# Macaron stack on one core: the routed experts' probability in the scattered row, and stack transfers issued one by one

## The reference

```python
logits = jnp.einsum('bsd,de->bse', x, router_w)
probs = jax.nn.softmax(logits, axis=-1)
topk_vals, topk_idx = jax.lax.top_k(probs, TOP_K)
top1_val = topk_vals[..., 0]
top1_idx = topk_idx[..., 0]
hid = jnp.einsum('bsd,edh->ebsh', x, up_w) * jax.nn.silu(jnp.einsum('bsd,edh->ebsh', x, gate_w))
mask = (top1_idx[None, :, :] == jnp.arange(Er)[:, None, None]).astype(x.dtype)
routed = jnp.einsum('ebsh,ehd,ebs->bsd', hid, down_w, mask)
...
return ALPHA * top1_val[..., None] * routed + shared
```

## Time and profile before

| | |
|---|---|
| median of 3 runs | 1754.54 us (1752.41 to 1758.84) |
| the profiled execution | 1754.69 us |
| span of its profile | 1752.7 us |
| PE busy | 1596.1 us, 91% |
| DVE busy | 969.2 us, 55% |
| ACT busy | 797.1 us, 45% |
| POOL busy | 343.7 us, 20% |
| stage m1 | 118 to 257 us of the span |
| guarded attention | 296 to 567 us |
| stage m2 | 568 to 700 us |

### The profile page before, as it was taken

How to read it: one execution, slowest core, us unless ns; L and a number is a source line. 1 busy time by engine, 2 the same in 40 slices (tenths; PEclk the granted TensorE clock), 3 DMA queues, 4 the chain that set the end, 5 groups by cost and what they waited for, 6 DMA issues and landing times. The chain is left out here.

```text
span 1752.7 us, 34539 instructions
## 1 busy us (share of the span) xinstructions
PE 1596.1 (91%) x13629; PEld 913.5 (52%) x13633; DVE 969.2 (55%) x2195; ACT 797.1 (45%) x1302; POOL 343.7 (20%) x489
## 2 busy tenths in 40 slices
PE   7979987899998998999789988999789986979998
PEld 2445654454553665445544554666434434755665
DVE  7674347887783333634563434545734446763455
ACT  5643333476675332432133334222588865643221
POOL 1313232132323322300330014000500000132000
PEclk9988998999999899999899989999999998989999
DMA  4633025111101411000000013564231004415563
GB/s 114 238 114 119 19 54 159 48 49 40 32 30 71 157 43 41 1 0 1 1 0 1 1 32 78 123 140 95 62 92 46 26 1 119 118 33 118 124 143 76
DMA packets 56305, 120.83 MB, mean 69 GB/s; under 512 B 8487, under 2 KB 35143, under 8 KB 51347
## 3 DMA queue, kind: packets, MB, share of 16 engines
q1 hardware_dynamic: 53676, 113.55, 24.1%
q0 software_dynamic: 2432, 5.00, 0.8%
q10 hardware_dynamic: 39, 0.07, 0.0%
HBM read 85.38 MB, written 19.96 MB: 60 GB/s over the span
## 5 line engine op out<-in xcount | busy, mean ns | idle before, releaser
L2512 DVE TENSOR_REDUCE a_most<-psum 128x1 f32<-128x512 f32 (+3 forms) x304 | 181.4, 654 | 45.4 <-PE psum L2142 44.2
L3407 ACT ACTIVATE t_silu<-psum 128x512 f32<-128x512 f32 x136 | 81.2, 597 | 258.2 <-PE psum L3467 257.1
L2470 ACT ACTIVATE a_probs<-psum 128x512 f32<-128x512 f32 (+1 forms) x304 | 153.9, 584 | 91.9 <-PE psum L2142 90.4
L3484 PEld LDWEIGHTS psum<-t_slot,t_hid 128*128 128x128 f32 x1024 | 131.0, 192 | 55.9 <-issue 44.7
L2773 ACT ACTIVATE ga_probs<-psum 128x1024 f32<-128x1024 f32 (+2 forms) x160 | 137.1, 954 | 19.4 <-PE psum L2142 18.8
L3583 DVE TENSOR_TENSOR t_prod<-t_silu,psum 128x512 f32<-128x512 f32 x104 | 71.4, 686 | 134.6 <-ACT t_silu L3407 125.2
L3484 PE MATMUL psum<-t_slot,t_hid 128*128 128x128 f32 x1024 | 132.0, 275 | 4.3 <-DVE t_hid L3574 4.3
L3467 PE MATMUL psum<-xnT,t_slot 128*128 128x512 f32 x256 | 131.3, 595 | 3.1 <-ACT t_silu L3407 3.1
L2142 PE MATMUL psum<-a_ks,a_qs 96*32 96x512 bf16 (+3 forms) x1536 | 123.9, 340 | 10.9 <-issue 5.6
L3472 PE MATMUL psum<-xnT,t_slot 128*128 128x512 f32 x256 | 130.7, 592 | 0.0
L2142 PE MATMUL psum<-a_qs,a_ks 128*32 128x512 bf16 (+3 forms) x1536 | 116.6, 330 | 5.4 <-ACT a_probs L2470 2.3
(11 more groups left out here) (455 smaller groups left out, 2996.7 us busy)
## 6 DMA issues: line engine op xcount, KB each, us to landing
t_spread<-factors SPq DMA_DIRECT2D x64, 512.0 KB, 6.4
m_experts<-experts_dram SPq DMA_DIRECT2D x14, 768.0 KB, 9.5
c_halves<-xnT SPq DMA_DIRECT2D x48, 128.0 KB, 2.3
t_slot<-experts_dram SPq DMA_DIRECT2D x32, 192.0 KB, 5.2
a_qs<-scratch_q SPq DMA_DIRECT2D x16, 288.0 KB
a_ks<-scratch_k SPq DMA_DIRECT2D x24, 192.0 KB
ga_qs<-scratch_q SPq DMA_DIRECT2D x16, 288.0 KB
la_qs<-scratch_q SPq DMA_DIRECT2D x16, 288.0 KB
```

The source lines that it names most:

```text
L2470: act.activation(probs[:, (n * BLOCKS + b) % PROBS, h0:h0 + heads, 0:wide], src, ACT.Exp, scale=SCALE).then_inc(probs_ready, 1)
L2512: v.tensor_reduce(most[:, row, h0:h0 + heads, qt % KPH], src, AX.X, ALU.max).then_inc(max_read, 1)
L3407: act.activation(silu[:, n % 2, :], core.psum[:, g_bank(n), :], ACT.Silu).then_inc(silu_ready, 1)
L3484: ins = pe.matmul(core.psum[:, c, t * P:(t + 1) * P], left[:, t * P:(t + 1) * P], weights, start=pair < 0 and t == 0, stop=False, skip_gro ...
```

## The change

Routed stages:

- the row of `xn_row` and of the sorted array gets a word more (130), and the coefficient is made before the scatter and stored in that column; the block's eviction multiplies by it. The scatter carries the coefficient with the row; `coef` is gone.
- the exponentials go ahead of all Silus on ACT, and the four small DVE instructions between the choice and the counting of the ranks.
- on PE, `shared_up(0)` is taken apart: gate product, ranks, up product.
- a join is one add of a whole chunk (128x512).

Guarded attention: `load` can issue some of its five transfers. For stacks 3 to 7, the two query transfers are issued where all five were, when units 0 and 6 of group n-1 are done; the three key transfers behind `maximum(n, 0)`, each behind a wait for unit 16, 22 and 28 of group n-1.

```diff
-ROW = D + 1
+ROW = D + 2
...
     def join(self, v, c):
...
         v.wait_ge(k.routed_in[c], 16 * (self.call + 1))
-        for t in range(TPC * c, TPC * (c + 1)):
-            xs = k.x[:, t, :]
-            v.scalar_tensor_tensor(xs, k.routed[:, t, :], k.coef[:, t:t + 1], xs, ALU.mult, ALU.add).then_inc(self.joined, 1)
+        tiles = slice(TPC * c, TPC * (c + 1))
+        v.tensor_tensor(k.x[:, tiles, :], k.x[:, tiles, :], k.routed[:, tiles, :], ALU.add).then_inc(self.joined, 1)
...
+            act.wait_ge(shifted, 1)
+            act.activation(prob[:, :, :], logit[:, :, :], ACT.Exp).then_inc(exps, 1)
             for n in range(SHARED):
                 gate(n)
-            act.wait_ge(shifted, 1)
-            act.activation(prob[:, :, :], logit[:, :, :], ACT.Exp).then_inc(exps, 1)
...
-            shared_up(0)
+            shared_gate(0)
             ranks()
+            shared_upper(0)
             for n in range(1, 2 * HT):
                 shared_up(n)
...
+            v.wait_ge(exps, 1)
+            v.wait_ge(chosen_ready, 1)
+            s.did(v.tensor_scalar(share[:, :], chosen[:, E - 1, :], -1.0, 1.0, ALU.mult, ALU.add))
+            s.chain(v.tensor_reduce(total[:, :], prob[:, :, :], AX.X, ALU.add))
+            s.chain(v.reciprocal(total[:, :], total[:, :]))
+            s.chain(v.tensor_tensor(core.xn_row[:, :, D + 1], share[:, :], total[:, :], ALU.mult))
+
             v.wait_ge(ranks_pe, 1)
...
-                    v.tensor_copy(outs[:, k - 2, :], core.psum[:, DOWN[(FRONT + k) % 2], 0:D]).then_inc(out_read, 1)
+                    v.tensor_scalar(outs[:, k - 2, :], core.psum[:, DOWN[(FRONT + k) % 2], 0:D], rows[:, k - 2, D + 1:D + 2], None, ALU.mult).then_inc(out_read, 1)
...
+    EARLY_PIECES, LATE_PIECES = ((0, 0), (1, 6)), ((2, 16), (3, 22), (4, 28))
...
+            def pieces(n, some):
+                for piece, u in some:
+                    sp.wait_ge(score_pe, (n - 1) * UNITS + u)
+                    stacks.load(sp, n + 1, (piece,))
+
             for n in range(1, GROUPS):
                 if RING <= n + 1 < GROUPS:
-                    sp.wait_ge(score_pe, (n - 1) * UNITS)
-                    stacks.load(sp, n + 1)
+                    pieces(n, EARLY_PIECES)
                 maximum(n, 0)
+                if RING <= n + 1 < GROUPS:
+                    pieces(n, LATE_PIECES)
                 maximum(n, 1)
```

More of the change, by code:

```diff
@@ L91, in __init__ @@
         self.spare = self.sb(ctx, "spare", [P, NT + 8])
-        self.coef = self.sb(ctx, "coef", [P, NT])
         self.mhalf = self.sb(ctx, "mhalf", [P, NT])
@@ L166, in statistics @@
         if self.call is not None:
-            v.wait_ge(self.joined, TPC * (c + 1 - self.ahead))
+            v.wait_ge(self.joined, c + 1 - self.ahead)
         for t in tiles:
@@ L943, in top1_stage @@
         total = core.sb(ctx, tag + "total", [P, NT])
+        share = core.sb(ctx, tag + "share", [P, NT])
         count = core.sb(ctx, tag + "count", [P, E])
@@ L1079, in ranks, with shared_gate @@
                 pe.matmul(core.psum[:, RANKS, P:2 * P], core.c("ones"), picks, start=True, stop=True).then_inc(ranks_pe, 1)
-            def shared_up(n):
+            def shared_gate(n):
                 c, j = divmod(n if n < SHARED else n - BLOCKS, HT)
@@ L1088, in shared_up, with shared_upper @@
                 pe.matmul(core.psum[:, GATE[n % 2], :], shared[:, GATE_AT + j * P:GATE_AT + (j + 1) * P], xc, start=True, stop=True).then_inc(gate_pe, 1)
+            def shared_upper(n):
+                c, j = divmod(n if n < SHARED else n - BLOCKS, HT)
+                xc = core.xnT[:, c * CH:(c + 1) * CH]
                 if 2 <= n < EARLY + 2:
@@ L1093, in shared_up @@
                 pe.matmul(core.psum[:, UP[n % 2], :], shared[:, UP_AT + j * P:UP_AT + (j + 1) * P], xc, start=True, stop=True).then_inc(up_pe, 1)
+            def shared_up(n):
+                shared_gate(n)
+                shared_upper(n)
             def shared_down(c):
@@ L1224, in _ @@
             v.tensor_scalar(table[:, :], owner[:, :], float(E - 2), None, ALU.min).then_inc(table_ready, 1)
[L1226 to L1231, removed]
             def multiply(n, dst):
@@ L1268, in _ @@
                     shared_add(c - 2)
-            coefficients()
             shared_add(1)
@@ L1291, in join @@
                 v.wait_ge(core.routed_in[c], 16 * (call + 1))
-                for t in range(TPC * c, TPC * (c + 1)):
-                    xs = core.x[:, t, :]
-                    v.scalar_tensor_tensor(xs, core.routed[:, t, :], core.coef[:, t:t + 1], xs, ALU.mult, ALU.add).then_inc(joined, 1)
+                tiles = slice(TPC * c, TPC * (c + 1))
+                v.tensor_tensor(core.x[:, tiles, :], core.x[:, tiles, :], core.routed[:, tiles, :], ALU.add).then_inc(joined, 1)
             join(0)
             if later:
-                v.wait_ge(joined, TPC)
+                v.wait_ge(joined, 1)
                 ahead_norm.statistics(v, 0)
@@ L1761, in spill, with load @@
                 sp.dma_start(dst, self.parts[1][k * rows:(k + 1) * rows, :, step % 2, :]).then_inc(self.spilled[1][step % 2], 16)
-    def load(self, sp, n):
+    def load(self, sp, n, pieces=range(5)):
         slot, parts = n % self.ring, self.PARTS
@@ L1768, in load @@
         rows = parts * parts * HD
-        for half in range(HALVES):
+        for half in [i for i in pieces if i < HALVES]:
             q = self.scratch[0][b, half, g * HD:(g + 1) * HD, :, :].rearrange("d i t -> (d i) t")
@@ L1773, in load @@
         k = self.scratch[1].rearrange("p b (g d h) t -> p d (b g) (h t)", d=HD, h=GROUP)
-        for p in range(parts):
+        for p in [i - HALVES for i in pieces if i >= HALVES]:
             if self.scratch[1].shape[2] == P:
```

## The result

The changed kernel takes 1742.34 us (median of 4 runs, 1741.21 to 1743.58) against 1753.47 us (4 runs, 1750.83 to 1758.84): a ratio of 0.9933 with a 95% interval of 0.9917 to 0.995, so 11.8 us less, and between 8.8 and 14.5. The forecast was 9.7 us less, with a range that holds the measured time.

The account below looks back on a forecast made before the run. TensorE, busy 91% of the span, was taken to bound the kernel. From 1754.69 us, 3.7 in the routed stages and 6.0 in the attention gave 1745.0 us; range 1741.0 to 1752.0.

Parts of the forecast that it names:

- Attention, 6.0 us: Guarded attention: smaller transfer bursts let late TensorE instructions through, closing holes for 4.6 us, plus 1.4 us of clock.
- The rule against it: Guarded attention: documentation says instruction block crossings are mostly hidden, so the gain would be 0 and the time 1751.0 us.
- m1 start, 2.4 us: First routed stage: rows arrive 1.1 us earlier, cutting TensorE's 2.42 us idle, and the kept clock saves 1.3 us more.
- The chain's own shift: Start of m1: ranks ahead of the first up product are read at 136.7 instead of 137.79, 1.1 us earlier.
- the cover of the coefficient chain: Start of m1: the added DVE instructions, 0.97 us, end at 136.22, ahead of the ranks at 136.7, costing nothing.
- the kept clock: First block of m1: with a shorter idle TensorE keeps its clock, 1.3 us gained; ends 0 and 1.3.
- m2 start, minus 0.35 us: Second routed stage: rows already hidden, so the earlier scatter gains nothing and the bare rank weight load costs 0.35 us.
- Block loop, nothing: Routed stages' 22 blocks: evicting by multiply instead of copy, and the row of 130 words, cost nothing.
- table load, 0.2 us in m2: Start of m2: the 1.28 us table load before the first block's Silu disappears, 0.2 us of it felt.
- Ends, 1.0 and 0.45 us: Ends of the routed stages: one wide add per join gains 1.0 us in m1 and 0.45 us in m2.
- Rival 3: Guarded attention: last key piece lands late, TensorE waits at the start of five groups, up to 1763.4 us; chance 0.06.
- Rival 2: Routed start gives nothing, because the DVE chain outlasts the ranks or the clock drops anyway; 1747.4 us, chance 0.12.

Follow-up runs that it names:

- burst_moved: The kernel before with the five back to back transfers of stacks 3 to 7 moved behind the first half's guard rows; 1746.8 us (0.9961).
- ranks_back: The changed kernel with the rank products behind the first up product again, all else as changed; 1742.92 us (0.9942).
- routed_only: The changed kernel with the guarded attention's stacks loaded as before, five transfers back to back; 1749.67 us (0.9985).

## Why the prediction was right, and where not

**The sum.** 9.7 us forecast, 11.8 measured (8.8 to 14.5), 9.1 by its halves. The chance for faster by over 0.5% was 0.43 and that is what came, with the end of the interval on that line. The terms as the traces have them, worked out below, add up to 9.4: 5.4 in the attention, 1.6 at the start of m1, 0.6 for the table load, 1.2 and 0.6 at the ends. That this stands so near 9.7 is partly luck: the start of m1 and the attention gave 1.4 us less than forecast, the ends and the table load 0.8 more, and a loss of 0.35 didn't come.

**Attention, 6.0 us.** The size holds. The window from the first probabilities to the choice of m2 is 268.8 us in the mean of four traces with the stacks loaded as before (266.8 to 271.0) and 263.4 in six with stacks 3 to 7 in pieces and stack 2 not (262.7 to 264.2); `burst_moved` has 264.9: 5.4 us. The reading that instructions were late, and that it was no data wait, holds. So does the step that the shorter burst lets the packet through. From 9 to 13 us behind the split of group 1 the kernel before moves 0.60 MB, the changed one 0.01 (364 to 368 us of the one, 356 to 360 of the other):

```profile
q1 hardware_dynamic: 172, 0.60, 42.8%
q8 instruction: 1, 0.02, 1.5%
...
q8 instruction: 1, 0.02, 1.8%
q1 hardware_dynamic: 64, 0.01, 1.2%
```

What failed is the sentence that it "ends some three microseconds earlier; the missing packet was late by about as much", as the account of what decides. One packet of the five was 3 us late, the others 0 to 1.3, and the length as such doesn't matter: the whole burst does no harm behind the guard rows, and harms in three groups of five at unit 14. What decides is whether large transfers are in flight in the microseconds ahead of one place in the group, where a packet is due 9.2 to 9.4 us behind the split. The change works because its query transfers are through by then and its keys start only at 12.3. I had seen that every hole stood "at the same instruction of the group" and used it only to exclude a data wait; it said that the place matters. Why it is this packet and not another that has no slack, no run shows.

**The rule against it.** The Trainium skill's page "Runtime: NRT & Kernel Launch", section "Instruction fetch mechanics", has the crossing of a code block mostly hidden, by which this part was worth nothing. The traces go against it at that one place and agree elsewhere: `burst_moved` has packets within its burst and no hole there.

**m1 start, 2.4 us.** The chain's own shift was right (1.15 us in the pair of traces above and 1.0 in the mean of all, for 1.1), and the cover of the coefficient chain and the kept clock came as forecast. Mis-sized was what the shift is worth: the idle of 2.42 us that it was to cut, and the low clock behind it (1.3 of the 2.4 us), needed a late scatter on top of the order of the program, and they are there in two of six traces. Choice to third transpose is 37.26 us in the mean of six old traces, 35.67 of eight new ones: 1.6 us in place of 2.4, and 0.7 where no scatter is late (36.37 in the mean of four). Between the two traces that I compare above it is 3.7 us. One trace can't tell a wait that repeats from one that happens.

**m2 start, minus 0.35 us.** The bare weight load doesn't show. Choice to third transpose of m2 is 36.28 us in the mean of six traces with the old order (35.7 to 36.7) and 36.37 of eight with the new one (35.4 to 36.9).

**Block loop, nothing; table load, 0.2 us in m2.** From the third transpose to the last product a stage takes 79.56 to 79.78 us in the twelve stages of six traces with the old routed code and 79.26 to 79.27 in sixteen of eight with the new one, `ranks_back` among them. The 0.3 us are there by the second block: its hidden transposes stand 4.38 us behind the third transpose in m2 before and 4.09 after, and the later blocks add nothing. TensorE has not made any block's output by then, so it is not the new eviction. What stood there on ACT and is gone is the table load in front of the first block's Silu. I had counted it in m2 alone, at 0.2 of its 1.28 us; 0.3 came, in both stages. That it is the table load is by exclusion; no run took it alone.

**Ends, 1.0 and 0.45 us.** 1.2 us in m1 (4.03 to 2.83; 4.04 to 2.88 in the means of six old and seven new traces). In m2 the statistics start 0.32 us ahead of the end of the last product in the mean of the six old traces, 0.96 ahead in the seven new ones: 0.64, where 0.45 was forecast. The join itself gives the 0.45; the other 0.2 I did not trace.

**Rival 3**, a late key piece, cost nothing even at unit 35, so its chance of 0.06 was not too low. **Rival 2** was half true: the start gave less than forecast in an ordinary execution, but not for either of its reasons.

**What was not forecast**: a wait of 0.7 to 0.85 us for a guard row, in three of the ten traces with the loads of stacks 3 to 7 moved. In the changed kernel the first of the three rows is issued at 405.80 and TensorE goes on at 410.84, 5.04 us later. Their issuing took 2.93 us, but it took 2.95 in `routed_only` (from 355.16) without a wait. The cause stays open.

## What to carry to other kernels

A hole without a releaser on a busy engine is worth a look at its instruction queue: write down when each packet lands, counted from a landmark of the loop, in a trace where it harms and in one where it doesn't. If one place of the loop is always the one to stop, move the large transfers away from the packet that feeds it; splitting them is only one way. Take the packet's end, from its share of the view, and not its start alone: the end sorted the cases that the start left mixed. And take a second trace of the kernel before ahead of pricing a wait: here the largest single term of one stage was built on a wait that two of six traces have.

## What the runs showed of the hardware

TensorE's instructions come in packets of 16 KB (1.82 MB in 111 for this execution), which the profile counts on the same 16 DMA engines as the data, one in four to eight microseconds in this stage. That q8 is TensorE's queue is a reading of the traces: it moves the most code, and TensorE resumes at a nearly fixed distance behind it. With a burst of 1152 KB in flight one of these packets came up to 3 us late (12.2 for 9.2), and TensorE resumed 1.2 to 1.6 us behind the end of the late packet each time (426.30 to 427.66 in the longest). The delay varies: in the same kernel the holes at that place were 0.41 to 2.33 us long. The end of a chain of 16 indirect scatters varied too, by 1.5 us, between executions of the same program; it was late in the two stages of 28 in which a TensorE packet started less than 2.0 us behind the start of the last scatter.

An add of two SBUF operands of 128x512 takes 0.69 us, as long as the multiply-add that reads PSUM; four of 128x128 take 0.90 us as adds and 1.14 us as multiply-adds with a coefficient for each partition.
